# Attention's MLP on one core: second gate product in the K projection's bank, third value product in the gates' bank, the norm's exponential behind the next square

## What is computed

```python
h = shift_token(x)
q, k, v = split(h @ wqkv)
q, k = l2norm(q) * qs, l2norm(k) * ksc
q, k = rotary_xpos(q, k)
x = x + local_attention(q, k, v) @ wo
h = shift_token(x)
mu, var = h.mean(-1), h.var(-1)
h = (h - mu) / sqrt(var + 1e-05) * lg + lb
a, g = split(h @ w1 + b1)
x = x + (a * gelu(g)) @ w2 + b2
```

## Time and profile before

| | |
|---|---|
| Median of 3 runs | 1152.17 us (1151.31 to 1152.67) |
| The profiled execution, its own time | 1143.62 us |
| Its span, first to last instruction | 1141.8 us |
| Busy: PE, DVE, ACT, POOL | 986.6, 730.8, 684.5, 518.0 us |

### The profile page before, as it was taken

How to read it: one execution, slowest core, us unless ns; L and a number is a source line. 1 busy time by engine, 2 the same in 40 slices (tenths; PEclk the granted TensorE clock), 3 DMA queues, 4 the chain that set the end, 5 groups by cost and what they waited for, 6 DMA issues and landing times.

```text
span 1141.8 us, 26074 instructions
## 1 busy us (share of the span) xinstructions
PE 986.6 (86%) x9072; PEld 626.4 (55%) x9072; DVE 730.8 (64%) x1689; ACT 684.5 (60%) x1325; POOL 518.0 (45%) x392
## 2 busy tenths in 40 slices
PE   4789999999998968689999999999828995855995
PEld 1445555555555347255555555555428983435995
DVE  1678678788776545377777867778674442665442
ACT  3567686686683562566766776674616664633662
POOL 2455556556442515355444543552463550264552
PEclk9999999999998987899999999999968998877998
DMA  5665554354434600354444444443332222012224
GB/s 177 162 159 140 120 145 113 91 134 112 96 93 98 81 1 3 86 119 112 99 108 95 112 94 94 113 106 82 133 108 57 67 72 78 18 45 65 67 68 129
DMA packets 89711, 109.99 MB, mean 96 GB/s; under 512 B 20368, under 2 KB 74384, under 8 KB 88816
## 3 DMA queue, kind: packets, MB, share of 16 engines
q1 hardware_dynamic: 82160, 91.17, 33.6%
q0 software_dynamic: 4544, 9.35, 2.4%
q10 hardware_dynamic: 2880, 7.81, 2.2%
HBM read 62.66 MB, written 12.07 MB: 65 GB/s over the span
## 4 chain that ended last, share of the span: by engine, by line
PE 67%; ACT 10%; issue 7%; DVE 7%; DMA 4%; POOL 4%; SPq 1%; ACTq 0%; DVEq 0%; POOLq 0%
PE banks L591 7%; PE banks L946 6%; PE banks L956 6%; PE banks L679 5%; PE banks L623 4%; PE banks L665 4%; PE banks L725 4%; PE banks L755 3%; PE banks L640 3%; PE banks L730 3%; PE banks L648 3%; PE banks L672 3%; ACT arena L1199 2%; PE banks L599 2%; PE banks L612 2%
## 5 line engine op out<-in xcount | busy, mean ns | idle before, releaser
L2084 POOL TENSOR_TENSOR arena<-arena 128x1024 f32<-128x1024 f32 x64 | 150.9, 2358 | 325.2 <-DVE arena L1677 319.4
L2073 POOL TENSOR_TENSOR arena<-arena 128x1024 f32<-128x1024 f32 x64 | 151.0, 2359 | 28.3 <-ACT arena L1194 28.0
L591 PE MATMUL banks<-arena 128*128 128x512 f32 x256 | 139.4, 632 | 6.3 <-DVE arena L1569 5.9
L1186 ACT ACTIVATE arena<-banks,arena 128x512 f32<-128x512 f32 x128 | 80.6, 679 | 101.5 <-PE banks L672 100.9
L1669 DVE TENSOR_REDUCE arena<-banks 128x4 f32<-128x512 f32 x128 | 82.5, 686 | 79.3 <-PE banks L623 78.7
L2063 POOL DMA_INDIRECT moe_outs<-arena x78 | 81.2, 1042 | 94.8 <-DVE arena L1926 87.2
L1412 ACT ACTIVATE arena<-banks,arena 128x128 f32<-128x128 f32 x312 | 89.0, 369 | 53.4 <-PE banks L946 53.1
L2056 POOL DMA_INDIRECT moe_rows<-arena x64 | 64.1, 1001 | 92.8 <-DVE arena L1650 67.6
L1677 DVE TENSOR_TENSOR arena<-arena 128x1024 f32<-128x1024 f32 x64 | 77.9, 1217 | 25.7 <-DMA arena<-arena 25.7
L956 PE MATMUL banks<-arena 128*128 x624 | 85.9, 280 | 3.0 <-ACT arena L1412 2.4
L946 PE MATMUL banks<-arena 128*128 128x128 f32 x624 | 85.6, 282 | 0.2 <-issue 0.2
(11 more groups left out here) (224 smaller groups left out, 1932.9 us busy)
## 6 DMA issues: line engine op xcount, KB each, us to landing
arena<-arena SPq DMA_DIRECT2D x256, 128.0 KB, 3.9
arena<-rstd SPq DMA_DIRECT2D x128, 256.0 KB, 4.1
arena<-moe_rows SPq DMA_DIRECT2D x78, 64.5 KB
arena<-in_mw SPq DMA_DIRECT2D x2, 2048.0 KB
arena<-moe_outs SPq DMA_DIRECT2D x16, 256.0 KB, 4.7
arena<-in_rot ACTq DMA_DIRECT2D x12, 256.0 KB, 3.3
arena<-in_wa ACTq DMA_DIRECT2D x2, 1026.0 KB, 6.6
arena<-ssm_a SPq DMA_DIRECT2D x4, 512.0 KB, 5.9
```

Of the source, the lines that this page charges most:

```text
L591: mm(bank[k], w_qkv[d][:, w0:w0 + P], (YA, YM)[d][:, c * C:(c + 1) * C], start=True, stop=True).then_inc(proj, 1)
L2073: nc.gpsimd.tensor_tensor(TA[:, n % 2], RAW, ROTV[:, :, 0, c * C:(c + 1) * C], ALU.mult).then_inc(cos_done, 1)
L2084: nc.gpsimd.tensor_tensor(TA[:, n % 2], TA[:, n % 2], TB, ALU.add).then_inc(rot_sum, 1)
```

## The change

It has two parts. The banks: `hidden` is split into `gate_product` and `value_product`, with the banks in `MLP_BANKS`; gate products go to banks 2, 1, 2 and value products to 7, 7, 2. Their order in step hp 1 becomes gate 0, value 0, gate 1, Q projection, gate 2, value 1, value 2. Gate 1 waits for ACT's copies of Q and K, gate 2 for the first gelu, value 1 for the first gating, value 2 for the third gelu. Whoever uses the banks next waits accordingly: the sum of squares of step hp 2 for the third gating, its output transposes for the second. The norm: `mlp_root` is split into `mlp_log`, where it was, and `mlp_exp`, which ACT now runs in the next step behind the square; DVE's `mlp_norm` moves to that step too, behind `rotate`. For the seventh chunk, whose norm falls in the last step, and for the eighth the norm and the banks stay as they were.

```diff
@@ -340,6 +340,7 @@
         LN_CEN, LN_VAR = (4, 6, 7, 7), (5, 5, 2, 2)
         LN_STEP = {1: 1, 4: 2, 5: 3}
         MLP_LAST = ((0, 5), (6, 7), (0, 5))
+        MLP_BANKS = ((2, 7), (1, 7), (2, 2))
         MX_TOK, MX_RANK = [(0, 3, 3, 7), (7, 7, 3, 7)], [(1, 4, 4, 6), (3, 4, 5, 4)]
         SN0 = 2 * NCH
         SN_ORDER = [(0, 0), (1, 0), (0, 1), (1, 1), (2, 0), (2, 1), (3, 0), (3, 1)]
@@ -353,6 +354,10 @@
 
             if n > 0:
                 eng.wait_ge(s, n)
+
+        def mlp_banks(g, j):
+
+            return MLP_LAST[j] if g == 2 * NCH - 1 else (2, 7) if g == 2 * NCH - 2 else MLP_BANKS[j]
 
         def bank2_read(eng, run, s):
 
@@ -363,7 +368,7 @@
                 if hp == 0 and 0 <= g - 2 < 2 * NCH:
                     return eng.wait_ge(mn_log, 2 * NCH * run + g - 1)
                 if hp == 1 and 0 <= g - 2 < 2 * NCH:
-                    return eng.wait_ge(gl_done, 3 * (2 * NCH * run + g - 1))
+                    return eng.wait_ge(hm_done, 3 * (2 * NCH * run + g - 1))
                 if hp == 2 and g < 2 * NCH:
                     return eng.wait_ge(v_evac, TILES * (2 * NCH * run + g + 1))
                 if hp == 3 and 0 <= g - 2 < 2 * NCH:
@@ -380,7 +385,7 @@
                 if hp == 0 and 0 <= g - 2 < 2 * NCH:
                     return eng.wait_ge(mn_copy, (2 * NCH - 1) * run + g - 1)
                 if hp == 1 and 0 <= g - 2 < 2 * NCH:
-                    return eng.wait_ge(hm_done, 3 * (2 * NCH * run + g - 1))
+                    return eng.wait_ge(hm_done, 3 * (2 * NCH * run + g - 2) + 2)
                 if hp == 2 and g < 2 * NCH:
                     return eng.wait_ge(v_evac, TILES * (2 * NCH * run + g + 1))
                 if hp == 3 and 0 <= g - 1 < 2 * NCH:
@@ -710,6 +715,30 @@
                     pe.wait_ge(mn_sq, gg + 1)
                     mm(bank[6][:], mean, MSQ, start=True, stop=True).then_inc(mn_var, 1)
 
+                def gate_product(g, s, j):
+                    d, gg = g // NCH, 2 * NCH * run + g
+                    k0, m = HBLK[j]
+                    if j == 0:
+                        pe.wait_ge(mn_out, gg + 1)
+                        pe.wait_ge(wm_in[d], 16)
+                        pe.wait_ge(ss_log, STEPS * run + s + 1)
+                    elif j == 1:
+                        pe.wait_ge(copied, 2 * (STEPS * run + s) + 2)
+                    else:
+                        pe.wait_ge(gl_done, 3 * gg + 1)
+                    mm(bank[mlp_banks(g, j)[0]][0:m, :], w1[d][:, HID + k0:HID + k0 + m], HN, start=True, stop=True).then_inc(g_mm, 1)
+
+                def value_product(g, s, j):
+                    d, gg = g // NCH, 2 * NCH * run + g
+                    k0, m = HBLK[j]
+                    if j == 0:
+                        pe.wait_ge(ot_evac, STEPS * run + s - 3)
+                    elif j == 1:
+                        pe.wait_ge(hm_done, 3 * gg + 1)
+                    else:
+                        pe.wait_ge(gl_done, 3 * gg + 3)
+                    mm(bank[mlp_banks(g, j)[1]][0:m, :], w1[d][:, k0:k0 + m], HN, start=True, stop=True).then_inc(a_mm, 1)
+
                 def hidden(g, s, j):
                     d, gg = g // NCH, 2 * NCH * run + g
                     k0, m = HBLK[j]
@@ -785,10 +814,13 @@
                     elif s in (4, 5):
                         first_norm(s - 2, s)
                     if hp == 1 and g >= 2:
-                        hidden(g - 2, s, 0)
+                        gate_product(g - 2, s, 0)
+                        value_product(g - 2, s, 0)
+                        gate_product(g - 2, s, 1)
                         project(s + 1, 0)
-                        hidden(g - 2, s, 1)
-                        hidden(g - 2, s, 2)
+                        gate_product(g - 2, s, 2)
+                        value_product(g - 2, s, 1)
+                        value_product(g - 2, s, 2)
                     if hp == 2:
                         project_v(g, s, 0)
                         project(s + 1, 0)
@@ -1212,7 +1244,7 @@
 
                 def gate(g, gg, j):
                     k0, m = HBLK[j]
-                    to, frm = (GL, 2) if g < 2 * NCH - 1 else (GL7, MLP_LAST[j][0])
+                    to, frm = GL if g < 2 * NCH - 1 else GL7, mlp_banks(g, j)[0]
                     if g == 2 * NCH - 1:
                         act.wait_ge(o_mm, 2 * STEPS * (run + 1))
                     act.wait_ge(g_mm, 3 * gg + j + 1)
@@ -1236,9 +1268,11 @@
                     after(act, a_mm, 3 * gg)
                     A(HN, bank[7][:], ACT.Copy).then_inc(mn_copy, 1)
 
-                def mlp_root(gg, frm=2):
+                def mlp_log(gg, frm=2):
                     act.wait_ge(mn_var, gg + 1)
                     A(MLT, bank[frm][:], ACT.Ln, bias=eps_c).then_inc(mn_log, 1)
+
+                def mlp_exp(gg):
                     act.wait_ge(mn_log, gg + 1)
                     A(MLT, MLT, ACT.Exp, scale=-0.5, bias=zero_c).then_inc(mn_rstd, 1)
 
@@ -1251,6 +1285,8 @@
                         evacuate_scores(n - 3)
                     if s < STEPS:
                         square(n)
+                        if hp == 1 and g >= 2:
+                            mlp_exp(gg - 2)
                         copy_out(s, n)
                         if hp == 0 and g >= 2:
                             evacuate_out(s - 4, n - 4)
@@ -1266,7 +1302,9 @@
                     if hp == 0 and g >= 2:
                         mlp_square(gg - 2)
                         mlp_copy(gg - 2)
-                        mlp_root(gg - 2)
+                        mlp_log(gg - 2)
+                        if s == STEPS:
+                            mlp_exp(gg - 2)
                     if hp == 1 and g >= 2:
                         for j in range(3):
                             gate(g - 2, gg - 2, j)
@@ -1301,7 +1339,8 @@
                 mlp_square(gg - 1, 5)
                 gate(6, gg - 2, 2)
                 log_exp_table()
-                mlp_root(gg - 1, 6)
+                mlp_log(gg - 1, 6)
+                mlp_exp(gg - 1)
                 if run:
                     tokens(0, 1)
                 else:
@@ -1699,7 +1738,7 @@
                     dve.wait_ge(gl_done, 3 * gg + j + 1)
                     dve.wait_ge(a_mm, 3 * gg + j + 1)
                     after(dve, w2_mm, gg)
-                    frm = 7 if g < 2 * NCH - 1 else MLP_LAST[j][1]
+                    frm = mlp_banks(g, j)[1]
                     STT(out=HM[0:m, j], in0=bank[frm][0:m, :], scalar=prm[0:m, 2 + j:3 + j], in1=(GL if g < 2 * NCH - 1 else GL7)[0:m, j],
                         op0=ALU.add, op1=ALU.mult).then_inc(hm_done, 1)
 
@@ -1758,6 +1797,8 @@
                         gate(g - 2, gg - 2, 2)
                     if s >= 1:
                         rotate(s - 1, n - 1)
+                    if gating:
+                        mlp_norm(g - 2, gg - 2)
                     if s >= 2:
                         maximum(n - 2)
                         subtract(n - 2)
@@ -1769,7 +1810,7 @@
                         gate(g - 2, gg - 2, 1)
                     if s in LN_STEP:
                         norm_chunks(norm0, shifted, [LN_STEP[s]])
-                    if hp == 0 and g >= 2:
+                    if s == STEPS:
                         mlp_norm(g - 2, gg - 2)
                     if hp == 2:
                         shift_v(gg)
```

## The result

The changed kernel is **slower by 3.2%**: 1187.6 us (median of 4 executions, 1176.88 to 1197.38) against 1151.74 us, a ratio of 1.032 (95% interval 1.027 to 1.036). The forecast was 1145.5 us.

The account below looks back on a forecast made before the run. PE, with two thirds of the span, was taken to bound the kernel. 12 x 0.40 + 1.9 = 6.7 us off the profiled 1143.62 gave 1136.9, carried to the median as 1145.5 us; range 1141.7 to 1149.8.

Parts of the forecast that it names:

- what hides the moved DVE part: Norm behind rotate: done at 630.15, before the first gate product could start at 630.4; cover 0.25 us.
- The slower rival: Norm behind rotate late for the first gate product through late transfers; up to 24 us lost, 1174 us; chance 0.05.
- The banks' part: Step 1's six products: second gate product no longer waits for the first gelu; 0.40 us per block, including 0.1 for the exponential.
- Value 0 to the transposes: Step 1 on PE: from first value product to transposes of the scores, some 5.4 us instead of 5.73.
- The first run's borders of 3.73 us: Borders to step 2, first run of the attention stage: earlier table load removes 0.38 us in five, 1.9 us together.
- The exponential's part: Border of steps 0 and 1: exponential behind the square saves 0.1 us per block on ACT; ends 0 and 0.42.
- The copy of the attention output: ACT's copy, for which the first value product waits, would begin at 630.81 instead of 630.92, 0.11 us earlier.
- The 0.4 us between gate 0 and value 0: Sign of being right: PE's wait moves to value 0, about 0.4 us between gate 0's end and it.
- the sum: Total gain over the kernel: 12 blocks x 0.40 us plus 1.9 us from the first run, 6.7 us.
- The rival of a standstill behind the table load: ACT stands still 1.28 us behind the table load, delaying the scores' exponentials; 1152 us, chance 0.01.

Follow-up runs that it names:

- the strided kernel: The changed kernel with DVE's second norm instruction walking even, then odd columns; 1172.8 us, ratio 1.023 to the kernel before.
- the banks alone: The kernel before with only the new banks, product order and their waits, exponential and norm left in place; 1142.5 us, ratio 0.994.
- the norm ahead of rotate: The changed kernel with DVE's norm put ahead of rotate instead of behind it; 1140.4 us, ratio 0.991 to the kernel before.
- the kernel with PE kept busy: The changed kernel with spare products on PE while it waits for the norm, results overwritten; 1172.5 us, ratio 1.020 to the kernel before.
- the norm alone: The kernel before with only the exponential and norm moved as in the change, old banks and product order; 1185.3 us, ratio 1.029.

## Why the prediction was wrong

**The step that failed** is the sentence on what hides the moved DVE part: "the exponential ends at about 628.9, the two instructions at 630.15". The exponential came on time, and rotate too. The two instructions took 5.2 us in a block of the second run instead of 1.25, since their durations came from a place where POOL was idle, and the new place is the one where rotate has just set POOL to work for 4.7 us. I looked at what the new place does to queues and semaphores, and not at who else runs there.

**The slower rival** had the right symptom (the first gate product waiting for the norm) and the wrong cause: rotate ended in time (653.01, with the square sum at 652.99), though it had waited 0.20 us for its transfer. A later transfer even helped where there was one: in the strided kernel rotate waited 0.42 to 0.65 us for it, the norm came ahead of POOL's sum and the block took 21.2 us instead of 26.1. Its price, each us of lateness past the cover costing 12 us over the blocks, was too low as well, as it knew nothing of the clock: 3.7 us of wait cost 6.5 us in a block of the second run (26.09 against 19.62), 2.8 of it at the lower level.

**The banks' part** was right in mechanism and low in size: 0.3 us for each block was forecast, the 0.1 of the exponential taken off, and with the banks alone it is 0.43 in the second run (20.23 to 19.80). Value 0 to the transposes was forecast as 5.42 us and measured 5.30 with the banks alone and 5.40 with the norm ahead of rotate. The first run's borders of 3.73 us became 3.35, as forecast.

**The exponential's part** was forecast as 0.1 us. Alone it is worth nothing; with the banks, where the second gate product no longer waits for the first gelu, it is worth 0.18 (19.80 to 19.62). The copy of the attention output came as reckoned, 5.59 us behind the transposes of step 0 instead of 5.68, but value 0 came 6.23 behind them instead of 6.52. It had not been waiting for that copy alone before: it started 0.96 us after gate 0, hardly more than a product takes, and gate 0 came earlier. The 0.4 us between gate 0 and value 0 that the prediction gave as a sign did not appear: value 0 follows after 0.94 us; gate 0 itself starts 1.95 us behind the square sum and not 1.8.

With the norm ahead of rotate, the twelve blocks are 9.3 us shorter together (5.6 in the first run, 3.7 in the second), where the sum was 6.7. So the rest of the working stands in its direction and was low in size, and one term with a wrong duration turned a gain of 0.9% into a loss of 3.2%.

**The rival of a standstill behind the table load** did not occur: the load's 1.28 us is followed at once by the next activation whenever its input is there.

## What to carry to other kernels

When an instruction moves, its duration doesn't move with it: look up what runs on the other engines at the new time, above all GpSimd beside VectorE, and ask of every row whose maximum is well above its median what the long ones ran beside. In this kernel the instruction that GpSimd waits for was a good one to stand in front of, and a bad one to stand behind. And price a wait of TensorE with what the clock may take behind it.

## What the runs showed of the hardware

- DVE and POOL held each other up for whole instructions: a 0.69 us instruction took up to 2.88 and a 0.55 us one 2.45 to 2.53 beside POOL's 2.36 us ones, and POOL's took up to 2.88 where DVE was first. The start decides: 0.04 us ahead was enough for the norm's first instruction (in the kernel with PE kept busy), and 0.04 us behind, in the change, too late.
- DVE instructions that read a PSUM bank kept their durations beside POOL (the subtract: 672 to 684 ns over 128 executions of the change).
- In the change, around waits of PE of 3.6 to 3.9 us, the granted clock over the step was 0.81 in all six blocks of the second run; around waits of 2.1 to 3.4 us in the first run, three blocks of six showed 0.89 and three 1.00. With the norm alone, two waits of 3.8 us showed 0.90. Around waits of 1.7 to 1.8 us, in the second run of the strided kernel, all showed 1.00. The length of the wait alone does not tell: the longest of the first run, 3.4 us, showed 1.00 and the shortest, 2.1 us, 0.89.
- A step of two columns left `tensor_scalar` on fp32 at 0.55 us for 128x512.
